# Attention head by head in two halves of the queries, with the row maxima half a head ahead

## What is computed

```python
scores = jnp.einsum('bhsd,bhed->bhse', q, k) * scale
attn = jax.nn.softmax(scores, axis=-1)
out = jnp.einsum('bhse,bhed->bhsd', attn, v)
```

## Time and profile before

| | |
|---|---|
| median of three runs | 1125.94 us |
| profiled execution, its own time | 1126.82 us |
| its span in the trace | 1125.0 us |
| TensorE busy in the span | 1006.5 us, 89% |
| VectorE, ScalarE busy | 839.2 us, 783.2 us |
| granted TensorE clock, mean | 0.954 of full |
| attention, first maximum to last copy | 371.3 to 980.4 us |

### The profile page before, as it was taken

One profiled execution on the slowest core, in us unless ns is written; L12 is line 12 of the kernel. 1 busy time (PEld: TensorE's weight loads), 2 busy tenths in 40 slices (PEclk: granted clock), 3 DMA queues, 4 the chain that ended last, 5 costly groups with the idle time before them and its releaser, 6 DMA issues.

```text
span 1125.0 us, 22107 instructions
## 1 busy us (share of the span) xinstructions
PE 1006.5 (89%) x8268; PEld 475.0 (42%) x8268; DVE 839.2 (75%) x1538; ACT 783.2 (70%) x1108; POOL 289.6 (26%) x296
## 2 busy tenths in 40 slices
PE   9846777798988789999999999999999999977994
PEld 6512223698954222332223222322233222247993
DVE  3599998426746789999999999999999995082213
ACT  3653433265545679999999999999999999821221
POOL 0078891674526300000000000000000000007762
PEclk9969998899989889999999999999999999988996
DMA  3055531754142221011110111011100100038623
GB/s 110 1 172 201 193 134 56 254 164 130 43 169 99 89 63 36 10 28 36 36 28 10 36 36 35 4 35 36 36 11 26 36 4 5 4 113 251 191 76 128
DMA packets 57973, 87.91 MB, mean 78 GB/s; under 512 B 26240, under 2 KB 28664, under 8 KB 57484
## 3 DMA queue, kind: packets, MB, share of 16 engines
q1 hardware_dynamic: 51694, 75.52, 21.6%
q0 software_dynamic: 4544, 9.32, 2.8%
q10 hardware_dynamic: 1630, 1.67, 0.5%
HBM read 73.10 MB, written 12.94 MB: 76 GB/s over the span
## 4 chain that ended last, share of the span: by engine, by line
PE 68%; DVE 12%; issue 8%; DMA 4%; ACT 4%; POOL 2%; SPq 1%; ACTq 0%; POOLq 0%; DVEq 0%
PE psum L987 24%; PE psum L973 22%; PE psum L1101 6%; PE psum L1121 4%; PE psum L977 2%; DVE tile_max L2060 2%; DVE ssm_h L1776 2%; PE psum L1081 1%; PE psum L817 1%; ACT hid L1422 1%; DMA q_stack<-max_parts 1%; PE psum L797 1%; POOL h0T L1505 1%; DVE ssm_g L1785 1%; PE psum L782 1%
## 5 line engine op out<-in xcount | busy, mean ns | idle before, releaser
L1360 ACT ACTIVATE probs<-psum 128x1024 f32<-128x1024 f32 x512 | 505.4, 1041 | 15.8 <-PE psum L977 4.8
L2060 DVE TENSOR_REDUCE tile_max<-psum 128x1 f32<-128x512 f32 x720 | 456.7, 685 | 28.0 <-PE psum L973 26.4
L973 PE MATMUL psum<-k_stack,q_stack 62*128 62x512 bf16 x994 | 311.2, 397 | 11.4 <-DMA q_stack<-q_dram 8.1
L987 PE MATMUL psum<-probs,v_head 128*32 128x256 f32 (+1 forms) x3840 | 320.4, 406 | 0.7 <-ACT probs L1360 0.4
L977 PE MATMUL psum<-q_stack,k_stack 64*128 64x512 bf16 x1024 | 302.6, 384 | 4.8 <-DMA q_stack<-max_parts 4.4
L973 PEld LDWEIGHTS psum<-k_stack,q_stack 62*128 62x128 bf16 x994 | 92.3, 110 | 245.5 <-DVE tile_max L2060 116.0
L1557 POOL TENSOR_TENSOR max_parts<-row_max,no_shift 128x8 bf16<-128x8 f32 x32 | 6.4, 200 | 538.2 <-DVE row_max L2036 538.2
L987 PEld LDWEIGHTS psum<-probs,v_head 128*32 128x32 f32 x3840 | 75.7, 108 | 154.4 <-issue 105.8
L1101 PE MATMUL psum<-x_cols,w1r 128*128 128x128 f32 (+1 forms) x624 | 81.8, 286 | 9.6 <-ACT hid L1422 4.6
L1101 PEld LDWEIGHTS psum<-x_cols,w1r 128*128 128x128 f32 x624 | 76.2, 199 | 12.5 <-ACT hid L1422 5.5
L1505 POOL TENSOR_TENSOR h0T<-dtuT,ssm_b 128x1024 f32<-128x1024 f32 x32 | 76.9, 2415 | 16.4 <-DVE ssm_h L1776 7.3
(11 more groups left out here) (289 smaller groups left out, 1070.0 us busy)
## 6 DMA issues: line engine op xcount, KB each, us to landing
w1r<-w SPq DMA_DIRECT2D x78, 256.0 KB, 3.6
ssm_b<-bc_dram SPq DMA_DIRECT2D x32, 512.0 KB, 4.1
k_stack<-k_dram SPq DMA_DIRECT2D x60, 120.0 KB
w_held<-w SPq DMA_DIRECT2D x16, 256.0 KB, 4.9
w1r<-y_dram SPq DMA_DIRECT2D x16, 256.0 KB, 5.1
q_stack<-q_dram SPq DMA_DIRECT2D x30, 96.0 KB
bc_p<-bc_dram SPq DMA_DIRECT2D x5, 512.0 KB, 5.5
xtok_dram<-x_tok SPq DMA_DIRECT2D x8, 256.0 KB, 2.4
```

Of the source, the lines that this page charges most:

```text
L973: mm(bank, queries, k_stack[rows, u, keys:keys + C], start=True, stop=True).then_inc(s1_ps, 1)
L987: i = mm(psum[32 * j:32 * j + VM, 7, lo:hi], v_head[:, u, kt, :], probs[:, kt % 4, j * C + lo:j * C + hi], start=kt == 0, stop=kt == KT - ...
L1360: f(probs[:, kt % 4, hf * HALF:(hf + 1) * HALF], banks(2 * slot, 2), ACT.Exp, scale=SCALE).then_inc(p_ready, 1)
L2060: v.tensor_reduce(top, bank, AX.X, ALU.max).then_inc(s1_read, 1)
```

## The change

A head is now worked through in two units of 16 entries, `entry(kt, hf) = 16*hf + kt`: all key tiles for one half of the queries, then all for the other. The maxima run 4 entries more than half a head ahead: entry `n` counted over the whole attention issues products `32 + 2*(n+4)` and the next, so those of a half end in entry 11 of the unit before its own. Ahead of the first entry stand 40 products of head 0, and only its first half is in the order of before. Values come in one call of 256 columns per entry, two entries behind their exponentials: none in entry 2 of a unit, two calls in entry 3 (key tiles 0 and 1), and those of the last two key tiles in entries 0 and 1 of the next unit. The exponentials' ring is eight entries instead of four key tiles (the same size). The copies take 128x256 of bank 7 after the second exponential of every unit; each is stored by five DMAs of half the size. TensorE waits for a half's rows before entry 0 of its unit. ScalarE issues head 0's first rows, SyncE all others, one half per unit, behind the store of the unit before; the initial loads of the heads 1, 2 and 3 are no longer broken by a row load.

```diff
-STORES = NC + 1
+QUARTER = C // 2
+STORES = 2 * (NC + 1)
+PROBS = 8
...
-FIRST_MAXIMA = first_order()
 MAXIMA = joined_order()
 SN = len(MAXIMA)
+UNIT = SN // 2
+FIRST_MAXIMA = first_order()[:UNIT] + MAXIMA[UNIT:]
...
 def entry(kt, hf):
-    return 2 * kt + hf
+    return KT * hf + kt
...
                 for h in range(NH):
-                    if h:
-                        store_head(h - 1)
-                    if h + 1 < NH:
-                        for hf in range(2):
-                            load_rows(sp, h + 1, (h + 1) % UN, hf)
+                    for hf in range(2):
+                        if h or hf:
+                            store(h - 1 + hf, 1 - hf)
+                        following = h + hf
+                        if following < NH:
+                            load_rows(sp, following, following % UN, 1 - hf)
                     if h + UN < NH:
                         sp.wait_ge(s2_ps, h * ENTRIES + ENTRIES)
                         load_q(sp, h + UN, h % UN)
                         load_k(sp, h + UN, h % UN)
-                store_last(NH - 1)
+                store(NH - 1, 1)
...
+                def values(h, hf, kt):
+                    n = h * ENTRIES + entry(kt, hf)
                     if kt == 0:
-                        pe.wait_ge(v_head_ready, h + 1)
-                        pe.wait_ge(o_copied, h + 1)
+                        if hf == 0:
+                            pe.wait_ge(v_head_ready, h + 1)
+                        pe.wait_ge(o_copied, 2 * h + hf + 1)
+                    pe.wait_ge(p_ready, n + 3)
                     for j in range(NC):
+                        i = mm(psum[32 * j:32 * j + VM, 7, unit_cols(hf)], v_head[:, h % UN, kt, :],
+                               probs[:, n % PROBS, j * QUARTER:(j + 1) * QUARTER], start=kt == 0, stop=kt == KT - 1, skip_group_check=True)
+                    i.then_inc(pv_done, 1)
+
+                def late_values(h, hf, kt):
+
+                    if kt < 2:
+                        if h or hf:
+                            values(h - 1 + hf, 1 - hf, KT - 2 + kt)
+                    elif kt == 3:
+                        values(h, hf, 0)
+                        values(h, hf, 1)
+                    elif kt > 3:
+                        values(h, hf, kt - 2)
+
+                def unit(h, hf):
+                    u = h % UN
+
+                    def ahead(kt):
+                        at = UNIT + 2 * (h * ENTRIES + entry(kt, hf) + LEAD)
+                        if at >= NH * SN:
                             return [lambda: None] * 2
...
+                        upper, lower = ahead(kt)
+                        upper()
+
+                        n = entry(kt, hf)
+                        if kt == 0:
+                            pe.wait_ge(rows_in[hf], h * ROW_LOADS + ROW_LOADS)
...
+                def keep(h, hf):
+
+                    act.wait_ge(pv_done, (2 * h + hf + 1) * KT + PROBS)
                     if hf == 0:
+                        act.wait_ge(o_stored[h % 2], 16 * STORES * (h // 2 + 1))
+                    f(o_sb[:, h % 2, unit_cols(hf)], psum[:, 7, unit_cols(hf)], ACT.Identity).then_inc(o_copied, 1)
...
-                load_rows(act, 0, 0, 1)
+                load_rows(act, 0, 0, 0)
...
-                        if p == SN // 2 + 1:
-                            row_maxima(hs, 0)
-                    row_maxima(hs, 1)
+                        if p % UNIT == UNIT - 1:
+                            row_maxima(hs, p // UNIT)
```

More of the change, by code:

```diff
@@ L986, in values @@
                     for j in range(NC):
[L987 to L1002, removed]
@@ L1009, in ahead @@
                             return [lambda: None] * 2
-                        return [lambda p=p: maxima(h + d, (u + d) % UN, p, turn + (u + d) // UN) for p in (2 * q, 2 * q + 1)]
+                        hs = at // SN
+                        return [lambda p=p: maxima(hs, hs % UN, p, hs // UN) for p in (at % SN, at % SN + 1)]
                     for kt in range(KT):
[L1013 to L1024, removed]
@@ L1025, in attention @@
-                for p in range(SN):
+                        upper, lower = ahead(kt)
[3 more added lines that the diff above has]
+                            pe.wait_ge(rows_in[hf], h * ROW_LOADS + ROW_LOADS)
+                        pe.wait_ge(p_ready, h * ENTRIES + (n + 1))
+                        scores(u, kt, hf, n % 2, 1)
+                        scores(u, kt, hf, n % 2, 0).then_inc(s2_ps, 1)
+                        lower()
@@ L1026, in attention @@
+                        late_values(h, hf, kt)
+                for p in range(UNIT + 2 * LEAD):
                     if p == FIRST_BANKS.index(1):
@@ L1028, in attention @@
                     maxima(0, 0, p)
-                for p in range(2 * LEAD):
-                    maxima(1, 1, p)
                 for h in range(NH):
-                    head(h, h % UN, h // UN, following=NH - 1 - h)
-                values(NH - 1, UN - 1, KT - 2, 1)
-                values(NH - 1, UN - 1, KT - 1)
+                    for hf in range(2):
+                        unit(h, hf)
+                values(NH - 1, 1, KT - 2)
+                values(NH - 1, 1, KT - 1)
             def attention_out():
@@ L1369, in attention @@
+                def keep(h, hf):
+                    act.wait_ge(pv_done, (2 * h + hf + 1) * KT + PROBS)
+                    if hf == 0:
+                        act.wait_ge(o_stored[h % 2], 16 * STORES * (h // 2 + 1))
+                    f(o_sb[:, h % 2, unit_cols(hf)], psum[:, 7, unit_cols(hf)], ACT.Identity).then_inc(o_copied, 1)
+                for p in range(UNIT + 1):
                     if FIRST_MAXIMA[p][3] == APART:
                         above(0, p)
-                above(1, 0)
@@ L1372, in attention @@
-                load_rows(act, 0, 0, 1)
+                load_rows(act, 0, 0, 0)
                 for h in range(NH):
-                    for kt in range(KT):
-                        ahead = h * SN + SN + 4 * kt + 2 * LEAD
-                        if ahead % GROUP == 0 and ahead < NH * SN:
-                            above(ahead // SN, ahead % SN)
-                        for hf in range(2):
-                            exponentials(h, kt, hf)
-                        if kt == 0 and h:
-                            keep(h - 1)
@@ L1382, in attention @@
-                keep(NH - 1)
-                act.wait_ge(o_copied, 1 + NH)
-                store_chunks(act, NH - 1, LAST_BY_ACT)
+                    for hf in range(2):
+                        for kt in range(KT):
+                            ahead = UNIT + 2 * (h * ENTRIES + entry(kt, hf) + LEAD)
+                            if ahead % GROUP == 0 and ahead < NH * SN:
+                                above(ahead // SN, ahead % SN)
+                            exponentials(h, hf, kt)
+                            if kt == 1 and (h or hf):
+                                keep(h - 1 + hf, 1 - hf)
```

92 lines of the change are left out of this document (41 added, 51 removed).

## The result

The changed kernel took 1169.24 us in the median of six runs (1165.67 to 1173.76), the kernel before, on the same chip, 1126.81 (1123.93 to 1129.06). The ratio is 1.038 (95% interval 1.035 to 1.041): slower by 42.4 us, inside the forecast range of 1148 to 1174 and 8 us above the forecast of 1161.2. The profiled execution took 1168.71 us with a span of 1166.9, against 1126.82 and 1125.0 before.

The account below looks back on a forecast made before the run. The prediction took TensorE's own instruction order as the bound, so its waits are paid in full. Terms 30.8 + 5.5 + 3.2 - 3.5 - 0.7 gave +35.3, so 1161.2 us against the median, range 1148 to 1174.

Parts of the forecast that it names:

- wait for the rows: At each unit's entry 0, TensorE waits for the rows of maxima, 0.93 us usually: +30.8 us (22 to 40).
- values in entries 2 and 3: Held maxima and two value calls in entry 3 make entry 4 of a unit 0.41 us late: +5.5 us.
- maxima half a head ahead: At the attention's end, only 20 entries instead of 36 run shorter without maxima beside them: +3.2 us.
- the start, earlier first entry: Head 0's first rows, issued by ScalarE, let entry 0 start at 395.7 instead of 400.4: -4.7 us.
- half clock: At the start, first values run at the 1.2 GHz level after TensorE stands: +1.2 us (0 to 3).
- the end: Behind the last exponential, fewer value calls and a smaller copy: -0.7 us.
- copies and stores: Half-size copies on ScalarE and 80 more store DMAs on SyncE fit into slack: 0.
- The allowance for late rows: In the row wait, the usual 0.93 us was taken as 1.05 to cover rows that come late.
- Rows in time: Rival: no wait at units' entry 0, the chain under 3.7 us, only the value pairs cost: 1128 us, chance 0.07.
- The faster rival: At entry 3 of a unit, rows in time and no maximum held: 1115 us, chance 0.03.
- Rows much later than forecast: Rival: stores and key loads delay every row load by 1 us or more beyond 1.05: 1194 us, chance 0.05.
- signs named: Expected trace: row DMA releases each unit's entry 0, units of 19.3 to 19.5 us, first entry near 395.7.

Follow-up runs that it names:

- e1: The changed kernel with maxima running 8 entries instead of 4 beyond half a head ahead: 1128.78 us, ratio 1.001 to the kernel before.
- e2: The changed kernel with a lead of 5 entries instead of 4: 1137.67 us, one run.
- e3: The changed kernel, lead still 4, row DMAs split between SyncE (side 0) and GpSimd (side 1): 1137.07 us, one run.
- e5: The changed kernel with lead 8 and plain reductions reading only 256 of 512 columns: 1119.49 us, one run.
- e4: The changed kernel with the first rows issued by SyncE between the loads of heads 1 and 2, instead of by ScalarE: 1156.32 us, one run.
- e8: e7 with bank 7 copied whole once per head (last head by halves), no empty value entry in second units: 1117.27 us, ratio 0.992 to the kernel before.
- e6: The kernel before the change with its lead cut from 4 entries to 2: 1171.1 us, one run.
- e7: The changed kernel with both lead 8 and first rows issued by SyncE between loads: 1122.54 us, ratio 0.996 to the kernel before.

## Why the prediction was right

The sign and the mechanism of the main term came out; the total was under-estimated by 7 to 8 us, since the wait, the start and the half clock all came out dearer than forecast. By the forecast's own terms, in us of the profiled execution:

| term | forecast | measured |
|---|---|---|
| wait for the rows | +30.8 | +35.0 |
| values in entries 2 and 3 | +5.5 | +4.1 |
| maxima half a head ahead | +3.2 | +3.2 |
| the start, earlier first entry | -4.7 | -2.4 |
| half clock | +1.2 | +4.7 |
| the end | -0.7 | -1.0 |
| copies and stores | 0 | no wait seen |

These give 43.6, and from the first maximum to the reciprocal behind the attention the trace has 43.6 us more than before. Outside the attention the two executions differ by -1.7 (1.9 later ahead of it, 3.6 less behind it), in code that the change doesn't touch. The span differs by 41.9.

**The wait for the rows.** The chain was read rightly: 4.57 us forecast, 4.63 measured, and the usual unit pays 19.24 - 18.33 = 0.91 us where 0.93 was worked out. The allowance for late rows, raising 0.93 to 1.05, was too small. The 29 units lose 566.5 - 29 x 18.325 = 35.1 us, less 1.4 of half clock, so 1.16 each; with 2.0 in the first unit and 1.9 in the last it is 37.6, less 2.6 paid before. The late ones are those of a head's second half: each of the heads 1 to 7 has one, by 0.4 to 1.25 us, and so have two later heads. The forecast had the lateness of three old heads to go by, and took it as rare. Their 36.83 us each were the mean of 36.98, 37.10 and an ordinary 36.40, and what showed there was only the part of the lateness beyond the 0.2 us to spare. e1 and e2 confirm the mechanism from the side of the lead, e3 from that of the issue: with four entries more the wait is gone, with one entry more or half of the issue time it is gone from the usual unit.

**Values in entries 2 and 3.** One unit of the kernel after, entries 0, 2, 3 and 4:

```profile
502.56 0.39 PE L979 MATMUL psum<-q_stack,k_stack 64*128 64x512 bf16 x2 [0.97 <-DMA q_stack<-max_parts]
...
504.79 0.40 PE L975 MATMUL psum<-k_stack,q_stack 62*128 62x512 bf16 x1
...
505.45 0.41 PE L975 MATMUL psum<-k_stack,q_stack 62*128 62x512 bf16 x1
...
506.05 0.40 PE L975 MATMUL psum<-k_stack,q_stack 62*128 62x512 bf16 x1
506.38 1.07 PE L990 MATMUL psum<-probs,v_head 128*32 128x256 f32 x16
507.39 0.40 PE L975 MATMUL psum<-k_stack,q_stack 62*128 62x512 bf16 x1
```

The forecast had the upper maximum of entry 3 at 2.91 us after entry 0, the lower at 3.51 and entry 4 at 4.90; they are at 2.89, 3.49 and 4.83. Two calls in a row take 1.01 us (506.38 to 507.39), not 1.05. e5 gives 0.35 us per unit for it: the step held, 0.05 us too large.

**The start** is the term whose size failed: the first entry and its half clock together were forecast at -3.5 (-8 to -1) and measured at about 0 (-2.4 and 2.3, less some 0.2 that before paid). ScalarE's row DMAs were taken at the 7.2 us of the earlier trace rows; they took 9.5. The same four, issued by ScalarE, took 7.3 in e2, 8.2 in e5, 8.5 in e1 and 9.3 in e3, so 7.2 was the short end of what these executions show. That no row load breaks SyncE's loads any more had been taken to bring the time down to 7.2 at worst; it grew instead, and e4, with a row load between them, gave 3.9. The other half is the clock. TensorE stood 10.25 us, and the 1.2 GHz level held until 407.6, 7.7 us past the first scores, and came once more for 3.4 us after a wait of 1.79 at 462. The first unit took 22.65 us: 18.33, 2.0 of waiting, 2.3 of half clock. The second dip cost 1.4. The third, at 1008, followed the 1.84 us of waiting ahead of the last unit: that unit takes 15.45 us from its first scores to its last exponential, and 14.26 in e4, which has the same wait and no dip, so 1.2 more. Less some 0.2 paid before, an estimate, that makes +4.7 instead of +1.2 (0 to 3).

**The rest.** A copy holds ScalarE 0.26 us, as the forecast's lower bound had it, and it costs nothing:

```profile
505.25 0.38 ACT L1367 ACTIVATE o_sb<-psum 128x256 f32<-128x256 f32 x1
505.51 1.95 ACT L1360 ACTIVATE probs<-psum 128x1024 f32<-128x1024 f32 x2
```

The end: 5.64 us from the last exponential to the reciprocal instead of 6.67.

**The rivals.** Rows in time, at 1128 us, is what e1 measured at 1128.78: the condition named for it, the chain against the distance from maxima to scores, is the one that decides; e1 meets it by the distance. That the two numbers lie so close is in part luck: the rival's sum has the same terms for the start and the values, whose sizes were off. The faster rival wanted rows in time and no held maximum; the first had to come from the lead, the second from less work for VectorE (e5) or another spread of the values (e8), and both of these are under the kernel before. Rows much later than forecast, at 1194, didn't come: the median landing is still 2.0 us. Of the signs named, the release by the row DMA stands at every unit, the usual unit takes 19.24 us, next to the 19.3 to 19.5 that were named, and the late ones lie above that; the first entry came at 398.0 in the times of before, not near 395.7.

## What to carry to other kernels

When work is reordered, count the distance from each product to its first use again, in time, and set the whole chain against it, the issue of every DMA in it included: here 4.6 us of chain had 3.7 us of distance, and a constant that had been enough for the old order lost 1 us per unit in the new one. TensorE paid this wait in full, and VectorE and ScalarE stood with it. Four more entries of lead took 40 us back (e1), a second issuing queue 32 (e3), with edits of a few lines. The reordering itself was worth nothing until the values were spread anew in it (e8).

## What was not expected of the hardware

**Issues that stretch.** The issue of one row DMA takes 0.6 us in the median, and now and then far more. Line L613 over the whole run, the kernel after (duration of one issue in ns, least, median, most), and the DMA queues from 537 to 540 us, beside the late issue above (packets, MB, share of 16 engines):

```profile
L613 SPq DMA_DIRECT2D q_stack<-max_parts x124: 477/601/1813, 417.6 to 1006.3; - x124
```

```profile
q1 hardware_dynamic: 144, 0.00, 2.8%
q8 instruction: 1, 0.02, 2.7%
```

One packet of about 16 KB of instructions was fetched in just that stretch. Of SyncE's issues of rows over 0.8 us, five of five before and nine of nine after overlap such a fetch, of the shorter ones 12 of 119 and 16 of 115. Over all eleven traces it is 51 of 51 and 126 of 1263. So a fetch and a long issue go together in these traces; that the one causes the other was not tried.

**The clock after short waits.** In e6, with two us of standing still per head, the clock was then granted at 1.2 GHz in eight of sixteen heads. After the change, with idle times of 0.5 to 1.8 us, it happened twice in 31 units, behind waits of 1.79 and 1.84 us, while the waits of 1.75 at 542 and 582 had no dip behind them, nor the 1.84 of e4. In e1, without waits, the mean from 404.5 to 967 us is 1.00. A head of e6 that met it lost 3.25 us where the others lost 2.29.

**DMAs behind bulk loads.** Four one-row DMAs were used 1.4 us after their last issue ended when they stood in SyncE's queue between loads (e4), as in the steady part (520.36 to 521.80 above), and 6.8 us after it when ScalarE issued them beside SyncE's loads (after). The longest landing on that line is 7.5 us. From the first issue to the first scores ScalarE's four took 7.3 to 9.5 us in the five runs that have them so (after, e1, e2, e3, e5), SyncE's 3.9 in e4, e7 and e8. That ScalarE's stood among the loads and SyncE's ahead of most of them is the other difference, and the two were not varied apart.
